# The mean square of y: two channel halves added on GpSimd ahead of the ones matmul

## The chip, the cores and the metric

The kernel runs on one core of a Trainium2 chip. The metric is the device time of one execution in microseconds (us); smaller is better. The core has five engines with queues of their own: TensorE (PE in the rows), VectorE (DVE), ScalarE (ACT), GpSimd (POOL) and SyncE (SP), which here issues transfers. Each works through its own list in order, and waits only where it meets a semaphore wait.

## The reference, cut to what matters

The input is 16 sequences of 512 tokens of 128 features. A layer with a state-space scan, a layernorm, a mixture of experts and a second layernorm follow one another. The change lies in the scan layer's own normalisation, the `rsqrt(mean(y * y))` below, a mean over 256 channels for each token:

```python
zxbcdt = x @ Win.T                         # z (256), xBC (512), dt (4)
xBC = silu(causal_conv4(xBC) + conv_b)     # x_ssm (256), B (128), C (128)
dtp = softplus(dt + dt_bias)
dA = exp(dtp * A)
# per token: h = dA * h + (dtp * x) outer B;  y = C . h + D * x
y = scan(...)                              # (b, 512, 256)
yn = y * rsqrt(mean(y * y, axis=-1, keepdims=True) + EPS) * norm_w
y = yn * silu(z)
x = layernorm(x + y @ Wout.T)
x = layernorm(x + moe(x))                  # 8 experts, top 2 of them per token
```

## The kernel before, in words

The program has a first part of about 510 us in which the sequences go through the scan layer and are sorted by expert, then the experts (`L575`, `L587` and others), then the last layernorm. Only the first part is touched.

It is a software pipeline over "slots", one per sequence `s`. A slot holds the scan of `s`, the projection and convolution of the next sequence `q`, the layernorm and routing of the one before, `r`, and the scatter of the rows of the one before that. Two slots at the start and four at the end are written out, and ten run in a hardware loop of two each. In a slot the work goes over `NC = 4` chunks `c` of 128 tokens. Every engine has its own function that writes its list for a slot: `slot_pe`, `slot_act`, `slot_dve`, `slot_pool`. The order on an engine is simply the order of that code.

Channels of y lie on the partitions, in `CC = 2` halves of 128, and tokens along the free axis: `yv` and `ysq` are [128, 2, tokens]. In chunk `c`:

- TensorE writes four heads' outputs to bank `p7` (L479, L485).
- VectorE adds the skip term and writes `yv` (L966). In the same row it does the conv taps (L794), the softplus steps on the small `sp` tiles (L812 to L832, spread over the chunks), the masked decay `M` (L856), `Xdt`, `carried` and `state`.
- ScalarE squares it to `ysq`: `square`, L638 to L642.
- GpSimd multiplies it by silu(z) to `gt`: `gate_y`, L1209 to L1215. It also makes `decayed` (L1238), `Xdd` (L1243) and `lhsA` (L1205, `expand`) for the scan, and issues one scatter of routed rows per chunk (L1221), whose descriptors it writes itself.

At the slot's end TensorE sums the squares over the channels: for each chunk, two matmuls of `ysq` halves with `ones`, accumulated in `p7` (L519 to L526). It then does the output projection from `gt` (L532) to `p5`, z (L408) and the projection of dt (L433). VectorE takes the mean of the squares to `ms` (L1010), after its gate steps `eg`, `gates`, top-8 and index. GpSimd raises `ms` to the power -1/2 (`rms`, L1262), issues four scatters more, and in the next slot does `lhsA` and then `rstd` (L1235), the layernorm's root. VectorE's `residual` (L878 to L900) waits for `rms` and the output projection.

Every float32 matmul shows in the trace as two passes, so that eight are x16.

Of the kernel before, what the change touches and what calls it, by code (L numbers as in the profile page):

```python
# [27 lines left out]
P = 128  # L28
SEQS, TOKS = 16, 512
NC = TOKS // P  # L30
H, HD = 4, 64
DI = H * HD
CC = DI // P
# [5 lines left out]
PADN = 96  # L39
# [28 lines left out]
def wait(eng, sem, value):  # L68

    if not isinstance(value, int) or value > 0:  # L70
        eng.wait_ge(sem, value)


def build(nc, t, out):
    ctx = ExitStack()
    with ctx:
        def sb(name, shape, dt=F32):
            return ctx.enter_context(nc.sbuf_tensor(name, shape, dt))
# [4 lines left out]
        def sem(name):  # L83
            return ctx.enter_context(nc.semaphore(name))
# [25 lines left out]
        ones = sb("ones", [P, P])  # L110
# [33 lines left out]
        carried = sb("carried", [P, DI])  # L144
        yv = [sb(f"yv{i}", [P, CC, P]) for i in range(2)]
        ysq = sb("ysq", [P, CC, TOKS])
        gt = sb("gt", [P, CC, TOKS])
        ms = sb("ms", [P, NC])
        rms = sb("rms", [P, NC])
# [82 lines left out]
        (x1_ready, Gm_ready, M_ready, Xdt_ready, v_ready, yv_ready, state_ready, sp_step, a_ready,  # L232
         tap_done, conv_done, carried_ready, ln_step, ve_ready, shift_ready, u_ready, gate_step, chosen_ready,
         ms_ready, pos_step, rank_read, slot_ready) = [sem(n) for n in names_dve]
        names_pool = ("lhsA_ready", "Xdd_ready", "decayed_ready", "g_ready", "rms_ready", "rstd_ready")
        (lhsA_ready, Xdd_ready, decayed_ready, g_ready, rms_ready, rstd_ready) = [sem(n) for n in names_pool]
        scattered = [[sem(f"scattered_{'AB'[k]}{i}") for k in range(2)] for i in range(2)]
        table_step = sem("table_step")
        table_ready = sem("table_ready")
# [146 lines left out]
        def _(pe):  # L386
# [50 lines left out]
            def slot_pe(s, scan, project, route):  # L437
# [79 lines left out]
                                       start=True, stop=True)  # L517
                    mm.then_inc(sums_psum, 1)
                if scan:  # L519
                    pe.wait_ge(sq_done, NC * (s.n + 1))  # L520
                    pe.wait_ge(yv_ready, NC * (s.n + 1))
                    for c in range(NC):
                        for k in range(CC):
                            mm = pe.matmul(p7[:, c * PADN:(c + 1) * PADN], ysq[:, k, c * P:(c + 1) * P],
                                           ones[:, 0:PADN], start=(k == 0), stop=(k == CC - 1))
                    mm.then_inc(ss_psum, 1)  # L526
                if scan:
                    pe.wait_ge(g_ready, NC * (s.n + 1))
# [89 lines left out]
        def _(act):  # L618
# [18 lines left out]

            def square(s, c):  # L638
                act.wait_ge(yv_ready, NC * s.n + c + 1)
                wait(act, ss_psum, s.n)  # L640
                act.activation(ysq[:, :, c * P:(c + 1) * P], yv[c % 2][:, :, :],
                               ACT.Square).then_inc(sq_done, 1)  # L642

# [523 lines left out]
        def _(pool):  # L1167
# [41 lines left out]
            def gate_y(s, c):  # L1209
# [4 lines left out]
                pool.tensor_tensor(gt[:, :, c * P:(c + 1) * P], yv[c % 2][:, :, :],  # L1214
                                   sz[s.par][:, :, c * P:(c + 1) * P], ALU.mult).then_inc(g_ready, 1)  # L1215

            def scatter(q, c, k):

                if (c, k) == (0, 0):
                    wait_apart(pool, slot_ready, q.n + 1)  # L1220
                pool.indirect_dma_start(  # L1221
                    out=sorted_rows[:, :],
                    out_offset=bass.IndirectOffsetOnAxis(slot[q.par][:, c, k:k + 1], 0),
                    in_=(rowA, rowB)[k][q.par][:, c, :], in_offset=None).then_inc(scattered[q.par][k], 16)

            def slot_pool(s, scan, project, route):
# [4 lines left out]
                for c in range(NC):  # L1231
                    n = NC * s.n + c
                    if route and c == 0:
                        pool.wait_ge(ve_ready, r.n + 1)
                        pool.tensor_tensor(rstd[:, :], ve[:, :], neg_half[:, :], ALU.pow).then_inc(rstd_ready, 1)  # L1235
                    if scan and 0 < c < NC - 1:
                        pool.wait_ge(state_ready, (NC - 1) * s.n + c)
                        pool.tensor_tensor(heads(decayed[:, :]), heads(state[(c - 1) % 2][:, :]),  # L1238
                                           per_head(decays[s.par][:, 2, :], c), ALU.mult).then_inc(decayed_ready, 1)
                    if scan and c + 1 < NC:  # L1240
                        pool.wait_ge(Xdt_ready, n + 1)
                        wait(pool, state_psum, (NC - 1) * s.n + c - 1)
                        pool.tensor_tensor(heads(Xdd[c % 2][:, :]), heads(Xdt[c % 2][:, :]),  # L1243
                                           per_head(decays[s.par][:, 1, :], c), ALU.mult).then_inc(Xdd_ready, 1)
                    if c > 0 and scan and (c + 2 < NC or project):
                        if c + 2 >= NC:
                            pool.wait_ge(a_ready, q.n + 1)
                        expand(n + 2, c + 2, s.par if c + 2 < NC else q.par)
                    if scan and c > 0:
                        gate_y(s, c - 1)  # L1250
                    if scatters:
                        scatter(s.plus(-2), c, 0)
                if project and not scan:
                    pool.wait_ge(a_ready, 1)
                    expand(0, 0, 0)
                    expand(1, 1, 0)
                if scan:
                    gate_y(s, NC - 1)
                    pool.wait_ge(ms_ready, s.n + 1)
                    if not (isinstance(s.n, int) and s.n < 1):  # L1260
                        pool.wait_ge(x1_ready, NC * s.n)
                    pool.tensor_tensor(rms[:, :], ms[:, :], neg_half[:, :], ALU.pow).then_inc(rms_ready, 1)  # L1262
# [83 lines left out]
```

## Time and profile before

| | us |
|---|---|
| median of three runs | 887.83 (886.22 to 889.96) |
| the profiled execution, whole | 882.78 |
| its span, first to last instruction | 880.9 |

| engine | busy us | share of the span |
|---|---|---|
| TensorE, matmuls | 708.9 | 80% |
| VectorE | 673.7 | 76% |
| GpSimd | 507.1 | 58% |
| ScalarE | 475.2 | 54% |

Busy time is an average over the whole program. The mean granted clock of TensorE was 0.932 of full speed. A row of the timeline gives an instruction's start, its duration, its engine and line, and what it writes from what it reads; in brackets stand the idle time of the engine before it and what ended it. The duration counts from when an instruction began to be executed, so that one held up within its execution shows as long and not as waiting.

### The profile page before, as it was taken

To read this page: it belongs to the slowest core of one execution; us is meant where nothing else is said; L and a number is where in the kernel's file an instruction comes from. 1 tells how busy PE (TensorE), PEld (TensorE's weight loads), DVE (VectorE), ACT (ScalarE), POOL (GpSimd) and SP (SyncE) were. 2 spreads that over 40 slices of the span, in tenths; PEclk is the share of its full clock that TensorE was granted. 3 is DMA by queue.
4 is the path that set the end of the run, shared out by engine and by line. 5 is a ranking of instruction groups with operands and counts; after the bars stand their busy time and mean duration, and the time that the engine had idled before them with its cause. 6 is when DMAs were issued, how large, how long until landed. Compare 5 with 4: busy or idle time off the path is not lost.

```text
span 880.9 us, 22802 instructions
## 1 busy us (share of the span) xinstructions
PE 708.9 (80%) x5288; PEld 601.1 (68%) x5289; DVE 673.7 (76%) x2331; ACT 475.2 (54%) x1188; POOL 507.1 (58%) x555
## 2 busy tenths in 40 slices
PE   5799878889988887897888731999999999999500
PEld 2577657667766665675666531999999999999500
DVE  5489988998998898898889645666666666667485
ACT  2566557546646655664665410655555555555355
POOL 2245666666665766676665755355555555555464
PEclk8899999999999999999999965999999999999855
DMA  3700011011101101101110002222222222222297
GB/s 85 251 26 23 16 43 44 14 42 45 42 14 43 42 12 42 42 21 36 31 35 14 19 30 73 59 64 61 66 65 64 68 61 63 65 57 77 72 301 218
DMA packets 74781, 53.84 MB, mean 61 GB/s; under 512 B 9435, under 2 KB 70110, under 8 KB 74480
## 3 DMA queue, kind: packets, MB, share of 16 engines
q1 hardware_dynamic: 56400, 31.90, 13.1%
q0 software_dynamic: 8448, 16.93, 5.9%
q10 hardware_dynamic: 9888, 4.49, 1.8%
q8 instruction: 19, 0.31, 0.1%
q14 instruction: 26, 0.21, 0.1%
HBM read 31.11 MB, written 22.69 MB: 61 GB/s over the span
## 4 chain that ended last, share of the span: by engine, by line
PE 36%; POOL 27%; issue 20%; DVE 9%; ACT 2%; DMA 2%; DVEq 1%; ACTq 1%; SPq 1%; POOLq 1%
PE pl L575 14%; POOL sorted_rows L1221 12%; PE p L587 12%; POOL lhsA L1205 5%; POOL gt L1214 4%; PE pj L569 2%; POOL rstd L1235 2%; ACT sz L745 2%; DVE acc L794 1%; DVE M L856 1%; PE pl L416 1%; POOL Xdd L1243 1%; POOL rms L1262 1%; DVE sp L822 1%; PE p L479 1%
## 5 line engine op out<-in xcount | busy, mean ns | idle before, releaser
L1275 POOL DMA_INDIRECT moe_rows<-yv,xs x136 | 146.0, 1074 | 141.0 <-DVE yv L1096 118.9
L724 ACT ACTIVATE L<-pl,b_sb 128x128 f32<-128x128 f32 x544 | 155.4, 369 | 118.9 <-PE pl L575 118.9
L575 PE MATMUL pl<-Btok,M 128*128 128x128 f32 x1088 | 151.2, 282 | 1.1 <-DVE M L1084 0.5
L587 PE MATMUL p<-w,L 128*128 x1088 | 143.9, 275 | 1.3 <-ACT L L724 1.3
L794 DVE SCALAR_TENSOR_TENSOR acc<-pj,conv_w_sb,acc 128x511 f32<-128x511 f32 (+2 forms) x192 | 142.2, 741 | 2.2 <-ACT acc L666 0.8
L575 PEld LDWEIGHTS pl<-Btok,M 128*128 128x128 f32 x1088 | 133.7, 193 | 4.4 <-DVE M L1084 3.2
L587 PEld LDWEIGHTS p<-w,L 128*128 128x128 f32 x1088 | 132.4, 192 | 1.8 <-issue 1.8
L1221 POOL DMA_INDIRECT sorted_rows<-rowA,slot x64 | 66.5, 1038 | 58.0 <-DVE token_id L875 47.5
L1080 DVE COPY Btok<-pj 128x128 f32<-128x128 f32 x136 | 39.7, 292 | 78.2 <-PE pl L575 61.2
L666 ACT ACTIVATE acc<-pj,conv_b_sb,conv_w_sb 128x512 f32<-128x512 f32 x64 | 49.8, 778 | 86.6 <-PE pj L397 85.8
L1205 POOL TENSOR_TENSOR lhsA<-after,a 128x512 f32<-128x512 f32 x64 | 67.9, 1062 | 32.0 <-DVE a L836 20.0
L416 PE MATMUL pl<-upto,lhsA 128*128 128x128 f32 x512 | 73.4, 290 | 0.8 <-POOL lhsA L1205 0.8
L1221 POOL DMA_INDIRECT sorted_rows<-rowB,slot x64 | 63.6, 994 | 18.0 <-issue 18.0
L397 PE MATMUL pj<-xT,w_xbc 128*128 128x512 f32 x128 | 69.1, 624 | 3.7 <-DVE acc L794 3.7
L416 PEld LDWEIGHTS pl<-upto,lhsA 128*128 128x128 f32 x512 | 67.9, 203 | 3.0 <-POOL lhsA L1205 1.6
L479 PEld LDWEIGHTS p<-M,Xdt 128*64 128x64 f32 x512 | 27.3, 136 | 60.4 <-issue 37.9
L631 ACT ACTIVATE L<-pl 128x512 f32<-128x512 f32 x64 | 38.2, 597 | 45.7 <-PE pl L416 44.5
L569 PE MATMUL pj<-ident,xs 128*128 128x128 f32 x136 | 40.1, 295 | 23.3 <-DMA xs<-sorted_rows 20.8
L1084 DVE COPY M<-w 128x512 f32 x136 | 57.2, 421 | 0.2 <-issue 0.2
L468 PE MATMUL p<-state,xc 128*128 128x256 f32 x96 | 33.5, 433 | 29.0 <-DVE state L976 23.3
L1214 POOL TENSOR_TENSOR gt<-yv,sz 128x256 f32<-128x256 f32 x64 | 53.3, 833 | 5.2 <-DVE yv L966 4.8
L856 DVE TENSOR_TENSOR M<-L,Gm 128x512 f32<-128x512 f32 x64 | 50.9, 795 | 2.0 <-ACT L L631 0.9
(170 smaller groups left out, 1477.3 us busy)
## 6 DMA issues: line engine op xcount, KB each, us to landing
xs<-sorted_rows SPq DMA_DIRECT2D x136, 65.0 KB, 1.8
xa<-in_x SPq DMA_DIRECT2D x16, 256.0 KB, 3.4
xres<-in_x SPq DMA_DIRECT2D x16, 256.0 KB, 3.0
w<-in_w SPq DMA_DIRECT2D x2, 2048.0 KB, 10.0
acc<-moe_rows SPq DMA_DIRECT2D x16, 256.0 KB, 3.9
xc<-moe_rows SPq DMA_DIRECT2D x16, 256.0 KB, 4.9
out<-sz ACTq DMA_DIRECT2D x16, 256.0 KB, 4.9
moe_rows<-yv,xs POOLq DMA_INDIRECT x136, 2.3
```

Of the source, the lines that this page charges most:

```text
L397: pe.matmul(pj[k % 2][:, :], w_xbc[:, k * P:(k + 1) * P], xT[q.par][:, :], start=True, stop=True).then_inc(proj_psum, 1)
L416: mm = pe.matmul(pl[c % 2][:, h * P:(h + 1) * P], lhsA[c % 2][:, h, :], upto[:, :], start=True, stop=True)
L569: pe.transpose(pj[k % 2][:, 0:P], xs[k][:, 0:P], ident[:, :]).then_inc(sT_psum, 1)
L575: mm = pe.matmul(pl[k % 2][:, f * P:(f + 1) * P], w1e[k % 2][:, f * P:(f + 1) * P], sT[k % 2][:, :], start=True, stop=True)
L587: mm = pe.matmul(o[:, 0:P], hT[k % 2][:, f, :], w2[:, bass.ds(e, 1), f, :].rearrange("p e d -> p (e d)"), start=(f == 0), stop=(f == FB - 1))
L724: act.activation(hT[k % 2][:, f, :], pl[k % 2][:, f * P:(f + 1) * P], ACT.Gelu, bias=b1[:, bass.ds(e * FB + f, 1)]).then_inc(hT_ready, 1)
L794: ins = dve.scalar_tensor_tensor(out=acc[:, k, j:TOKS], in0=pj[k % 2][:, 0:TOKS - j], scalar=conv_w[:, k, TAPS - 1 - j:TAPS - j], in1=acc[ ...
L856: dve.tensor_tensor(M[c % 2][:, :, :], L[c % 2][:, :, :], Gm[:, c, :].unsqueeze(1).broadcast_to([P, H, P]), ALU.mult).then_inc(M_ready, 1)
L1205: pool.tensor_tensor(lhsA[c % 2][:, :, :], after[:, :].unsqueeze(1).broadcast_to([P, H, P]), a[par][:, (c % NC) * H:(c % NC + 1) * H].unsq ...
L1214: pool.tensor_tensor(gt[:, :, c * P:(c + 1) * P], yv[c % 2][:, :, :], sz[s.par][:, :, c * P:(c + 1) * P], ALU.mult).then_inc(g_ready, 1)
L1221: pool.indirect_dma_start(out=sorted_rows[:, :], out_offset=bass.IndirectOffsetOnAxis(slot[q.par][:, c, k:k + 1], 0), in_=(rowA, rowB)[k][ ...
L1275: pool.indirect_dma_start(out=moe_rows[:, :], out_offset=bass.IndirectOffsetOnAxis(xs[k][:, P:P + 1].bitcast(I32), 0), in_=ye[k % 4], in_o ...
```

## The change

A new tile `ysum` holds the sum of the two halves of `ysq`. GpSimd makes it, one add of 128x128 per chunk (`add_halves`). It waits for the square of that chunk, and for TensorE to have read the `ysum` of the sequence before. In chunks 1 to 3 the add of the chunk before comes after `gate_y` and ahead of the scatter; for the last chunk it comes ahead of `gate_y`. TensorE has one matmul per chunk over `ysum` in place of two over `ysq`, and waits for GpSimd's semaphore instead of ScalarE's. `square` waits until GpSimd has read the `ysq` of the sequence before. Lines behind the new code have moved by 1 to 8.

```diff
@@ slot_pe
                 if scan:
-                    pe.wait_ge(sq_done, NC * (s.n + 1))
+                    pe.wait_ge(sq_sum, NC * (s.n + 1))
                     pe.wait_ge(yv_ready, NC * (s.n + 1))
                     for c in range(NC):
-                        for k in range(CC):
-                            mm = pe.matmul(p7[:, c * PADN:(c + 1) * PADN], ysq[:, k, c * P:(c + 1) * P],
-                                           ones[:, 0:PADN], start=(k == 0), stop=(k == CC - 1))
+                        mm = pe.matmul(p7[:, c * PADN:(c + 1) * PADN], ysum[:, c * P:(c + 1) * P],
+                                       ones[:, 0:PADN], start=True, stop=True)
                     mm.then_inc(ss_psum, 1)
@@ square
-                wait(act, ss_psum, s.n)
+                wait(act, sq_sum, NC * (s.n - 1) + c + 1)
@@ gpsimd
+            def add_halves(s, c):
+                tok = slice(c * P, (c + 1) * P)
+                pool.wait_ge(sq_done, NC * s.n + c + 1)
+                wait(pool, ss_psum, s.n)
+                pool.tensor_tensor(ysum[:, tok], ysq[:, 0, tok], ysq[:, 1, tok], ALU.add).then_inc(sq_sum, 1)
+
...
                     if scan and c > 0:
                         gate_y(s, c - 1)
+                        add_halves(s, c - 1)
                     if scatters:
                         scatter(s.plus(-2), c, 0)
...
                 if scan:
+                    add_halves(s, NC - 1)
                     gate_y(s, NC - 1)
```

GpSimd's list before, from chunk 1 of a slot in the loop to the end of that slot. `decayed`, `Xdd` and `lhsA` belong to the scan, `gt` is y gated, and the DMA is a scatter:

```order
L1238 TENSOR_TENSOR decayed<-state,decays 128x256
L1241 REGISTER_ALU
L1243 TENSOR_TENSOR Xdd<-Xdt,decays 128x256
L1205 TENSOR_TENSOR lhsA<-after,a 128x512
L1212 ISA
L1214 TENSOR_TENSOR gt<-yv,sz 128x2x128
L1221 DMA sorted_rows<-rowA,slot 67584x130
...
L1205 TENSOR_TENSOR lhsA<-after,a 128x512
L1214 TENSOR_TENSOR gt<-yv,sz 128x2x128
L1221 DMA sorted_rows<-rowA,slot 67584x130
L1214 TENSOR_TENSOR gt<-yv,sz 128x2x128
L1262 TENSOR_TENSOR rms<-ms,neg_half 128x4
```

The same part of GpSimd's list now:

```order
L1244 TENSOR_TENSOR decayed<-state,decays 128x256
L1247 REGISTER_ALU
L1249 TENSOR_TENSOR Xdd<-Xdt,decays 128x256
L1205 TENSOR_TENSOR lhsA<-after,a 128x512
L1212 ISA
L1214 TENSOR_TENSOR gt<-yv,sz 128x2x128
L1221 TENSOR_TENSOR ysum<-ysq 128x128
L1227 DMA sorted_rows<-rowA,slot 67584x130
...
L1227 DMA sorted_rows<-rowA,slot 67584x130
L1221 TENSOR_TENSOR ysum<-ysq 128x128
L1214 TENSOR_TENSOR gt<-yv,sz 128x2x128
L1270 TENSOR_TENSOR rms<-ms,neg_half 128x4
```

In each of chunks 1 to 3 `ysum` stands between `gt` and the scatter, and at the end it stands between the last scatter and the last `gt`. Nothing else changes place on GpSimd. TensorE's list at the end of a slot, before:

```order
L516 MATMUL p<-a,ones 128x96
L524 MATMUL p<-ones,ysq 128x96 x8
L532 MATMUL p<-w_out,gt 128x128 x8
L407 REGISTER_ALU
L408 MATMUL pj<-xT,w_z 128x512
```

and now:

```order
L517 MATMUL p<-a,ones 128x96
L524 MATMUL p<-ones,ysum 128x96 x4
L532 MATMUL p<-w_out,gt 128x128 x8
L408 REGISTER_ALU
L409 MATMUL pj<-xT,w_z 128x512
```

Eight matmuls have become four in the same place. VectorE's list is the same as before.

## Rows read from the trace of the kernel before

**Rows 1.** Busy us of each engine, 113 to 485 us: span, PE, PEld, DVE, ACT, POOL
```profile
113.00:485.00 372.00, 317.53 (x2227) 247.42 (x2226) 331.95 (x1079) 217.03 (x432) 247.31 (x277) 0.98 0.11 33
```

**Rows 2.** Timeline, end of one slot: start us, duration us, engine, line, out<-in [idle before]
```profile
230.34 0.73 POOL L1214 TENSOR_TENSOR gt<-yv,sz 128x256 f32<-128x256 f32 x1
...
231.24 1.01 POOL L1221 DMA_INDIRECT sorted_rows<-rowA,slot  x1 [0.17 <-issue]
...
232.07 0.42 ACT L641 ACTIVATE ysq<-yv 128x256 f32<-128x256 f32 x1 [0.61 <-DVE yv L966]
...
232.28 0.74 POOL L1214 TENSOR_TENSOR gt<-yv,sz 128x256 f32<-128x256 f32 x1
...
232.58 1.99 PE L524 MATMUL p<-ones,ysq 128*128 128x96 f32 x16
232.61 0.46 DVE L989 TENSOR_SCALAR eg<-eg 128x32 f32<-128x32 f32 x1
...
235.57 0.14 DVE L1010 TENSOR_SCALAR ms<-p 128x4 f32<-128x4 f32 x1
...
235.79 1.04 POOL L1262 TENSOR_TENSOR rms<-ms,neg_half 128x4 f32<-128x4 f32 x1 [2.77 <-DVE ms L1010]
...
236.21 1.02 PE L408 MATMUL pj<-xT,w_z 128*128 128x512 f32 x2
```

**Rows 3.** The chain of waits, one sequence later: start us, us, what
```profile
274.28 1.05 POOL rstd L1235
```

**Rows 4.** One line's instructions: duration in ns, min/median/max, first and last start
```profile
L1289 POOL TENSOR_TENSOR xc<-acc x8: 453/456/843, 835.2 to 865.8; 128x128 f32<-128x128 f32 x8
```

**Rows 5.** Timeline, chunk 1 and the start of chunk 2 of the slot of rows 2
```profile
217.05 1.06 POOL L1221 DMA_INDIRECT sorted_rows<-rowA,slot  x1 [3.31 <-DVE token_id L875]
...
217.66 0.42 DVE L820 TENSOR_SCALAR sp<-sp 128x16 f32<-128x16 f32 x1
...
218.29 2.07 DVE L822 SCALAR_TENSOR_TENSOR sp<-sp 128x16 f32<-128x16 f32 x1
...
219.28 1.04 POOL L1205 TENSOR_TENSOR lhsA<-after,a 128x512 f32<-128x512 f32 x1
...
220.28 1.27 POOL L1214 TENSOR_TENSOR gt<-yv,sz 128x256 f32<-128x256 f32 x1
...
220.89 0.69 DVE L822 SCALAR_TENSOR_TENSOR sp<-sp 128x16 f32<-128x16 f32 x1
...
222.16 0.16 DVE L822 SCALAR_TENSOR_TENSOR sp<-sp 128x16 f32<-128x16 f32 x1
...
223.86 0.60 POOL L1238 TENSOR_TENSOR decayed<-state,decays 128x256 f32<-128x256 f32 x1 [1.14 <-DVE state L976]
```

**Rows 6.** Timeline, chunk 1 of another slot, VectorE
```profile
280.39 2.83 DVE L820 TENSOR_SCALAR sp<-sp 128x16 f32<-128x16 f32 x1
```

**Rows 7.** Timeline, chunk 0 of two slots
```profile
210.34 0.69 DVE L856 TENSOR_TENSOR M<-L,Gm 128x512 f32<-128x512 f32 x1
...
211.11 1.05 POOL L1205 TENSOR_TENSOR lhsA<-after,a 128x512 f32<-128x512 f32 x1
...
213.98 0.69 PE L493 MATMUL p<-Xdd,Btok 128*128 128x256 f32 x2 [1.78 <-POOL Xdd L1243]
...
241.69 1.83 DVE L856 TENSOR_TENSOR M<-L,Gm 128x512 f32<-128x512 f32 x1 [0.24 <-ACT L L631]
```

**Rows 8.** Timeline, end of the last sequence
```profile
508.17 0.17 DVE L989 TENSOR_SCALAR eg<-eg 128x32 f32<-128x32 f32 x1
...
508.34 0.71 POOL L1214 TENSOR_TENSOR gt<-yv,sz 128x256 f32<-128x256 f32 x1 [0.40 <-DVE yv L966]
508.37 0.35 DVE L994 RECIPROCAL gates<-eg 128x32 f32<-128x32 f32 x1
...
510.82 0.16 DVE L1010 TENSOR_SCALAR ms<-p 128x4 f32<-128x4 f32 x1 [0.86 <-PE p L524]
```

**Rows 9.** Busy us as in rows 1 in one microsecond; the last but two is the granted clock
```profile
215.00:216.00 1.00, 1.00 (x6) 1.00 (x6) 0.93 (x9) 0.45 (x2) 0.00 (x0) 0.50 0.00 0
```

More of the change, by code:

```diff
@@ L146, in build @@
         ysq = sb("ysq", [P, CC, TOKS])
+        ysum = sb("ysum", [P, TOKS])
         gt = sb("gt", [P, CC, TOKS])
@@ L234, in build @@
          ms_ready, pos_step, rank_read, slot_ready) = [sem(n) for n in names_dve]
-        names_pool = ("lhsA_ready", "Xdd_ready", "decayed_ready", "g_ready", "rms_ready", "rstd_ready")
-        (lhsA_ready, Xdd_ready, decayed_ready, g_ready, rms_ready, rstd_ready) = [sem(n) for n in names_pool]
+        names_pool = ("sq_sum", "lhsA_ready", "Xdd_ready", "decayed_ready", "g_ready", "rms_ready", "rstd_ready")
+        (sq_sum, lhsA_ready, Xdd_ready, decayed_ready, g_ready, rms_ready, rstd_ready) = [sem(n) for n in names_pool]
         scattered = [[sem(f"scattered_{'AB'[k]}{i}") for k in range(2)] for i in range(2)]
```

## The prediction

> **What bounds the kernel now.** I first read the busy time by stretch. In the scan, over the twelve sequences from 113 to 485 us, VectorE is busy 331.95 of 372 us, TensorE 317.53 and GpSimd 247.31 [rows 1]. So a removed matmul need not pay, and added GpSimd work looks cheap; only the order in time can tell. I therefore read the end of a sequence, then its chunk 1.
>
> The last ones matmuls of a sequence (L524) start at 232.58 and take 1.99 us, until 234.57. VectorE, which consumes their sum in `ms` (L1010), starts that at 235.57, a full microsecond later: it is in an unbroken row of conv taps and gate steps, of which `eg` at 232.61 is one. GpSimd then starts `rms` at 235.79, having been idle 2.77 us [rows 2]. So TensorE's sum is not what is late; VectorE's own row is. Behind `rms` the chain of waits runs on GpSimd without a hole: after `rms` come four scatters and `lhsA`, and then `rstd`, in the next sequence at 274.28 [rows 3]. When `ms` comes sets when all of this comes. The next two outputs, z and the projection of dt, hang on TensorE, but in the next chunk 0 it waits 1.78 us for GpSimd's `Xdd` anyway [rows 7].
>
> **The change part by part.** I follow the sequence whose `rms` starts at 235.79.
>
> *Removed from TensorE.* Half of 16 passes in 1.99 us: 0.124 us each, so 1.0 us per sequence, 16 us in all, where VectorE was 1.0 us behind [rows 2]. Price: nothing, except in the first and last sequence. In the last, `ms` did wait 0.86 us for L524 [rows 8]. There the sum now starts later by one add (about 0.5 us) and lasts 1.0 us less: 0.4 us to the good. In the first I take the same, an estimate from this row. Together -0.8 us.
>
> *Added to GpSimd.* 64 adds of 128x128. The nearest row is the add of two 128x128 tiles later in the program, 0.456 us [rows 4]; GpSimd's records overlap by some 0.04 us (`lhsA` ends at 220.32, `gt` starts at 220.28, rows 5), so each takes 0.41 us of its queue. From above, `gt` with twice the elements takes 0.73 us [rows 2]; I take the first, whose shape is the same. Behind each of the first three adds stands the scatter of that chunk, then the next chunk's `decayed`, `Xdd` and `lhsA`.
>
> *What the adds push on GpSimd.* After the add of chunk 0 `decayed` has 1.14 us of idle before it [rows 5], so nothing comes late there. In chunk 3 nothing is idle: `gt` at 230.34 becomes 230.72, as the add of chunk 1 precedes it. It ends at 231.45. The square of chunk 2 ends 0.61 us ahead of that of chunk 3, so at 231.46 [rows 2], and the add runs to 231.95. The scatter, which needs 0.17 us of issue and 1.01 us, runs from 232.09 to 233.10, the last add to 233.57 and the last `gt` to 234.27. The square that the last add needs ended at 232.49, so it is GpSimd's backlog that counts and not ScalarE.
>
> *What that does to the end.* The ones matmuls start at 233.65 in place of 232.58 and end at 234.64, as now. The out matmuls follow at 234.56, behind a `gt` that is done; z follows at 236.37 in place of 236.21. Residual needs both out (236.54) and `rms` (235.79 + 1.04 = 236.83), so `rms` still decides. GpSimd is free at 234.27 with `ms` due at 235.57: 1.3 of the 2.77 us of idle are left. TensorE gets a new hole of about 0.9 us ahead of the sum, which nobody waits for. The new waits are thus covered. If that cover were gone (an add of 0.73 us, so GpSimd later by 4 x 0.3 us), the sum would end at 235.8 and cost 0.3 us per sequence.
>
> *What the adds do to VectorE without any wait.* This is the part that the list of waits does not show. In chunk 1 a tiny `sp` step on 128x16 takes 2.07 us, where its kind takes 0.16. It starts at 218.29, beside GpSimd's `decayed`, and ends at 220.36, after `Xdd` and with the end of `lhsA` at 220.32. The next one, at 220.89, takes 0.69 us and ends at 221.58, with `gt` (221.55); and `gt` itself takes 1.27 instead of the 0.73 of rows 2, held by a VectorE operation in its turn [rows 5]. Ten of the sixteen sequences show the 2.07. In another, `sp` at 280.39 takes 2.83 us, until 283.22, through all four GpSimd operations from `decayed` to `gt` [rows 6]. So VectorE operations that read two SBUF tiles, or are of the copy and scalar kind, and GpSimd's tensor operations keep each other out. Taps and `yv`, which read PSUM, run at their usual 0.74 and 0.42 us beside GpSimd.
>
> The new add stands directly behind this `gt`, with `sp` waiting. At the border between two back-to-back GpSimd operations VectorE was passed over at `decayed`/`Xdd` and `Xdd`/`lhsA`, and let in at `lhsA`/`gt` [rows 5]; in the slot at 280 it was passed over at all three [rows 6]. If it is passed over here, `sp` ends 0.41 us later and with it the taps, `yv`, and VectorE's whole row down to `ms`; the little idle time that it has [rows 1] lies mostly ahead of chunk 1's `sp`, in chunk 0. If it is let in, the add lies beside the tap that follows `sp` and costs nothing. Bounds: 0 to 0.7 us. I take 0.41, since the short operations' borders were the ones that stayed shut. It applies in the fifteen sequences that have such `sp` steps: 15 x 0.41 = 6.2 us.
>
> The Trainium skill ("SBUF — State Buffer", section "Who interferes with whom") says that of the two engines "Whoever issues first gets the shared pair for the whole instruction", and that a VectorE operation with two SBUF inputs competes with a GpSimd operation that reads SBUF. The trace agrees on the kinds and the full blocking (2.07 us of rows 5). Taken as first come first served, it would give the add no right over an `sp` that has waited since 220.89, and the price would be zero; rows 6 speak against reading it so.
>
> At the end of the sequence the same lock is met by `eg` (L989): 0.46 us now, held until `gt` ends at 233.02 [rows 2], where 0.17 us is its bare time [rows 8]. In the changed kernel a scatter stands at 232.09 to 233.10 instead. A scalar-kind step that started 0.61 us into a scatter (217.66 against 217.05) was held to its end too, 0.42 us [rows 5], so I expect `eg` to end at 233.08, as now. The reciprocal behind it ran its 0.35 us inside a `gt` [rows 8] and is not held. Price 0, bounds -0.29 (`eg` gets through) to +1.2 (passed over until 234.27).
>
> **The sum.** +6.2 - 0.8 = +5.4 us. The profiled execution took 882.78 us (span 880.9), so 888.2; the median of the runs shown, 887.83, is 5.05 above it, and I forecast 893.2 on that scale. Everything behind 513 us is untouched.
>
> **Rivals.**
> *The add is hidden.* `sp` is let in ahead of it. Only -0.8 remains: 887.0. For it: the border `lhsA`/`gt`. Against: rows 6. The skill's rule above gives this time.
>
> *Faster.* `eg` gets through beside the scatter, VectorE's row shortens by 0.29 us in 14 sequences, and the add is hidden too: -4.1 - 0.8 = -4.9, 882.9. For it: the scatter starts only about 0.5 us before `eg`, earlier than in the held case. Against: it needs both, and TensorE, 0.16 us later than now, then presses on residual's other inputs.
>
> *A lost race in chunk 0.* `M` at 210.34 ends at 211.03, 0.08 us before `lhsA` at 211.11. Where `M` started at 241.69, only 0.22 us before `lhsA`, it took 1.83 us instead of 0.69, until 0.56 us behind `lhsA`'s 1.05, and GpSimd's `rstd` had to wait for it [rows 7]; four sequences have this. TensorE is 0.16 us later at z, and if G thereby comes late enough against GpSimd, most sequences pay about 0.5 us (those 0.56 less the usual overlap): some 10 more x 0.5 = 5 on top of the 5.4, or `eg` passed over to `gt`'s start (0.5 x 14 = 7): 898 to 901. Against: VectorE's row, later by 0.41, moves `rms` too, so TensorE is rather early by comparison.
>
> *TensorE's clock.* After the wait of 1.78 us for `Xdd` at 213.98 the granted clock read 0.50 at 215 to 216, the 1.2 GHz level [rows 7, 9]. Were the new 0.9 us hole to bring a fall, sum and out would take 3.0 us more per sequence, 2 of it past `rms`: +30 us on the forecast, 923. Against: the hole is half as long as that one, and TensorE has work on either side.
>
> **Chances.** Forecast 0.42, hidden 0.26, faster 0.12, lost race or `eg` 0.17, clock 0.03. The likeliest has its own range of 890 to 896. For all: 883 to 902. A difference of 0.5% (4.4 us) is about what a measurement of this kernel can tell from none: faster than 883.4 takes half of "faster" and a little of "hidden", 0.08; slower than 892.3 takes two thirds of the forecast, the race and the clock, 0.48; the rest is 0.44.
>
> **What would show it.** The `sp` after `M` in chunk 1 at 1.1 us instead of 0.69 (step right) or still 0.69 (hidden rival); the add at about 0.45 us; the last ones matmuls starting 1.1 us later against `yv`, still ahead of `ms`; GpSimd's idle before `rms` at 1.3 to 1.7 us instead of 2.77; `eg` at 0.4 to 0.5. From one `rms` to the next now 30.8 us, or 31.3; in the forecast 31.2 and 31.7. I am wrong if `ms` waits for TensorE in the middle sequences, if the period is unchanged, or if the granted clock of the scan falls.

## The result, and the profile after

| | before | changed |
|---|---|---|
| median | 887.36 us (886.22 to 889.96) | 898.97 us (898.64 to 899.57) |
| profiled execution, its span | 882.78, 880.9 us | 898.64, 896.7 us |
| mean granted clock | 0.932 | 0.929 |

The changed kernel is slower: ratio 1.0126, 95% interval 1.0106 to 1.0146, which is 11.6 us by the medians. The two profiled spans differ by 15.8 us, as that of before was at the low end of its runs. The forecast was +5.4 us, 893.2, with a whole range of 883 to 902 and a likeliest one of 890 to 896.

I cut each sequence (from the `rms` of the one before to its own) at two marks that every trace has: the starts of `decayed` in chunk 1 and in chunk 2. Summed over the twelve sequences from 3 to 14, counting the first as 0:

| stretch | before | changed | difference |
|---|---|---|---|
| `rms` to `decayed` of chunk 1 | 160.1 us | 162.5 | +2.35 |
| to `decayed` of chunk 2 | 69.4 | 73.6 | +4.22 |
| to the next `rms` | 143.2 | 149.7 | +6.51 |

These +13.1 us, 1.5 us in the other sequences and 1.3 us behind the scan make the 15.8. Each stretch has a cause of its own.

**The middle stretch** is the step that was forecast. Timeline of the changed kernel, chunk 1 and the start of chunk 2 of the slot whose `rms` comes at 242.16; the columns are as in rows 2:

```profile
224.11 0.63 POOL L1244 TENSOR_TENSOR decayed<-state,decays 128x256 f32<-128x256 f32 x1
...
224.26 2.75 DVE L822 SCALAR_TENSOR_TENSOR sp<-sp 128x16 f32<-128x16 f32 x1
...
226.25 0.72 POOL L1214 TENSOR_TENSOR gt<-yv,sz 128x256 f32<-128x256 f32 x1
...
226.93 0.68 DVE L856 TENSOR_TENSOR M<-L,Gm 128x512 f32<-128x512 f32 x1
226.94 0.98 POOL L1221 TENSOR_TENSOR ysum<-ysq 128x128 f32<-128x128 f32 x1
...
227.54 0.42 DVE L822 SCALAR_TENSOR_TENSOR sp<-sp 128x16 f32<-128x16 f32 x1
...
230.20 0.70 PE L469 MATMUL p<-state,xc 128*128 128x256 f32 x2 [2.37 <-DVE state L976]
230.24 0.60 POOL L1244 TENSOR_TENSOR decayed<-state,decays 128x256 f32<-128x256 f32 x1 [1.15 <-DVE state L976]
```

`sp` now takes 2.75 us, until 227.01, with the end of `gt` at 226.97. In rows 5 it took 2.07 and ended with `lhsA`. `M` then gets in ahead of the add, and it is the add that is held (0.98 us), as `gt` was before (1.27). In both kernels the second `sp` ends with the last operation of GpSimd's run, at 221.58 with `gt` before [rows 5] and now at 227.96 with the add (227.92), so VectorE's row is later by about the add's length. From `decayed` to `decayed` it is 6.13 us in all twelve sequences, where it was 5.73 in ten and longer already in two (5.81, and 6.28 with the `sp` of rows 6).

The row of TensorE is the one that I had not asked for. Its wait for `state` is 2.36 or 2.37 us in eleven of the twelve. In before it was at most 1.97, as in this row of that trace:

```profile
410.76 0.70 PE L468 MATMUL p<-state,xc 128*128 128x256 f32 x2 [1.97 <-DVE state L976]
```

**The last stretch** holds the largest sum. TensorE's rows from that wait on, first one slot earlier, then (behind the dots) in the slot shown above; after that the busy time of both by the microsecond, with the columns of rows 9, whose last but two is the granted clock:

```profile
197.21 0.70 PE L469 MATMUL p<-state,xc 128*128 128x256 f32 x2 [2.37 <-DVE state L976]
197.74 1.06 PE L398 MATMUL pj<-xT,w_xbc 128*128 128x512 f32 x2
198.73 1.12 PE L480 MATMUL p<-M,Xdt 128*64 128x128 f32 x8
199.78 1.23 PE L486 MATMUL p<-ident,carried 128*128 128x128 f32 x4
...
231.69 0.66 PE L480 MATMUL p<-M,Xdt 128*64 128x128 f32 x8
232.28 0.71 PE L486 MATMUL p<-ident,carried 128*128 128x128 f32 x4
```

```profile
198.00:199.00 1.00, 1.00 (x4) 0.27 (x4) 1.00 (x5) 0.16 (x1) 0.61 (x1) 0.80 0.00 0
199.00:200.00 1.00, 1.00 (x9) 0.67 (x8) 1.00 (x4) 1.00 (x3) 0.21 (x1) 0.50 0.00 0
...
232.00:233.00 1.00, 1.00 (x13) 0.83 (x8) 1.00 (x4) 1.00 (x3) 0.20 (x1) 1.00 0.00 0
```

The same hole of 2.37 us stands ahead of both. In one the clock then reads 0.50, the 1.2 GHz level, for some 3.4 us, and eight matmuls take 1.12 us instead of 0.66; in the other it stays at 1.00. The fall came in five of the twelve sequences. The last stretch of those is 13.25 to 13.50 us instead of 11.68 to 11.92: 1.57 each, 7.8 in all. In the profile of before no sequence has a fall in chunk 2.

Yet the clock fell there too, in five of the twelve sequences, each time between chunks 0 and 1, behind TensorE's waits for `M` or `Xdd`, as in rows 7 and 9. In three of the five it cost nothing (the sequence of rows 9 took 30.81 us, one without a fall 30.80); the other two are those whose middle stretch was longer already. The changed kernel has one fall in that place. It has six falls in all against five, and its mean clock is almost the same: the falls moved to where they cost time.

**The first stretch.** Timeline of a later slot, whose `rms` came at 273.62:

```profile
274.56 0.59 PE L409 MATMUL pj<-xT,w_z 128*128 128x512 f32 x1
...
278.44 0.69 DVE L908 TENSOR_TENSOR Gm<-p,upto 128x512 f32<-128x512 f32 x1 [0.20 <-PE p L449]
...
279.26 2.08 DVE L856 TENSOR_TENSOR M<-L,Gm 128x512 f32<-128x512 f32 x1
...
279.73 1.05 POOL L1205 TENSOR_TENSOR lhsA<-after,a 128x512 f32<-128x512 f32 x1
...
280.73 1.52 POOL L1241 TENSOR_TENSOR rstd<-ve,neg_half 128x4 f32<-128x4 f32 x1
```

z starts 0.94 us behind `rms`, where it was 0.42 [rows 2]. `Gm` waits for TensorE, and `M` starts 0.47 us ahead of `lhsA`, where it had 0.77 [rows 7]. It loses the contest with it: 2.08 us instead of 0.69, until 0.56 us behind `lhsA`'s end, and the stretch is 13.62 us instead of 13.15. Four sequences of before paid that, ten of the changed kernel do.

The end of the sequence in the first slot, and the end of the last sequence:

```profile
237.91 0.46 POOL L1221 TENSOR_TENSOR ysum<-ysq 128x128 f32<-128x128 f32 x1
...
238.53 1.01 POOL L1227 DMA_INDIRECT sorted_rows<-rowA,slot  x1 [0.15 <-issue]
...
238.98 0.53 DVE L989 TENSOR_SCALAR eg<-eg 128x32 f32<-128x32 f32 x1
...
239.56 0.47 POOL L1221 TENSOR_TENSOR ysum<-ysq 128x128 f32<-128x128 f32 x1
239.97 0.73 POOL L1214 TENSOR_TENSOR gt<-yv,sz 128x256 f32<-128x256 f32 x1
...
240.08 1.13 PE L524 MATMUL p<-ones,ysum 128*128 128x96 f32 x8 [0.97 <-POOL ysum L1221]
...
241.94 0.14 DVE L1010 TENSOR_SCALAR ms<-p 128x4 f32<-128x4 f32 x1
...
242.16 1.04 POOL L1270 TENSOR_TENSOR rms<-ms,neg_half 128x4 f32<-128x4 f32 x1 [1.46 <-DVE ms L1010]
...
525.36 0.16 DVE L1010 TENSOR_SCALAR ms<-p 128x4 f32<-128x4 f32 x1 [0.52 <-PE p L524]
```

Here the changed kernel is as forecast: the sum is ready at 241.21, `ms` does not wait for it, and GpSimd still has 1.46 us to spare. In the last sequence `ms` waits 0.52 us for TensorE instead of 0.86 [rows 8], but in a second execution of the changed kernel, below, it waits 0.86 again.

### The profile page after: what moved, and what is told of

The parts are those of the page before. It is cut to its first block, busy times and chain, and to the rows that moved or that the text cites. A ratio compares the mean times of both kernels' runs of the same rounds, so it can differ in the third digit from the quotient of the medians.

```text
span 896.7 us, 22670 instructions
## 1 busy us (share of the span) xinstructions
PE 702.8 (78%) x5160; PEld 588.9 (66%) x5161; DVE 689.6 (77%) x2331; ACT 476.2 (53%) x1188; POOL 537.9 (60%) x619
## 4 chain that ended last, share of the span: by engine, by line
PE 34%; POOL 28%; issue 21%; DVE 10%; ACT 3%; DMA 2%; DVEq 1%; ACTq 1%; SPq 1%; POOLq 1%
PE pl L575 14%; PE p L587 12%; POOL sorted_rows L1227 12%; POOL gt L1214 4%; POOL lhsA L1205 4%; POOL ysum L1221 3%; PE pj L569 2%; POOL rstd L1241 2%; ACT sz L745 2%; DVE M L856 1%; DVE acc L794 1%; POOL decayed L1244 1%; POOL rms L1270 1%; POOL Xdd L1249 1%; DVE sp L822 1%
## 5 line engine op out<-in xcount | busy, mean ns | idle before, releaser
L417 PE MATMUL pl<-upto,lhsA 128*128 128x128 f32 x512 | 70.6, 282 | 0.8 <-POOL lhsA L1205 0.8
L417 PEld LDWEIGHTS pl<-upto,lhsA 128*128 128x128 f32 x512 | 65.2, 196 | 2.9 <-POOL lhsA L1205 1.6
L856 DVE TENSOR_TENSOR M<-L,Gm 128x512 f32<-128x512 f32 x64 | 59.6, 931 | 2.0 <-DVE Gm L908 1.0
L480 PE MATMUL p<-M,Xdt 128*64 128x128 f32 x512 | 44.9, 298 | 18.0 <-DVE Xdt L933 17.2
```

What stands on the lines that cost most here:

```text
L417: mm = pe.matmul(pl[c % 2][:, h * P:(h + 1) * P], lhsA[c % 2][:, h, :], upto[:, :], start=True, stop=True)
L480: mm = pe.matmul(p7[half, (h // 2) * P:(h // 2 + 1) * P], Xdt[c % 2][:, h * HD:(h + 1) * HD], M[c % 2][:, h, :], start=(h < 2), stop=(c == ...
L856: dve.tensor_tensor(M[c % 2][:, :, :], L[c % 2][:, :, :], Gm[:, c, :].unsqueeze(1).broadcast_to([P, H, P]), ALU.mult).then_inc(M_ready, 1)
```

## The experiments

Each was timed beside the kernel before on the same chip. The first four shared a chip, on which before took 884.7 us.

**The adds without TensorE's part.** Against the changed kernel:

```diff
-                    pe.wait_ge(sq_sum, NC * (s.n + 1))
+                    pe.wait_ge(sq_done, NC * (s.n + 1))
-                        mm = pe.matmul(p7[:, c * PADN:(c + 1) * PADN], ysum[:, c * P:(c + 1) * P],
-                                       ones[:, 0:PADN], start=True, stop=True)
+                        for k in range(CC):
+                            mm = pe.matmul(p7[:, c * PADN:(c + 1) * PADN], ysq[:, k, c * P:(c + 1) * P],
+                                           ones[:, 0:PADN], start=(k == 0), stop=(k == CC - 1))
@@ square
+                wait(act, ss_psum, s.n)
```

> GpSimd makes the four adds per sequence as in the changed kernel, but nobody waits for them at the end: TensorE runs both ones matmuls per chunk over ysq, as before. Theory (the add holds VectorE's sp step at the shared port by 0.4 us in chunk 1, and the later state lengthens TensorE's hole in chunk 2, where its clock then falls): the chunk 1 step of 0.4 us per sequence is there, 893 if the clock does not fall in chunk 2 and up to 900 if it does; TensorE is not later at z, so M of chunk 0 does not lose against lhsA more often than in the kernel before. Rival (the loss comes from TensorE waiting for GpSimd at the end of a sequence): 887 to 889.

Measured 899.01 us, ratio 1.0128 (1.0086 to 1.0169): the whole loss without anything of TensorE's. `sp` is at 2.75 and the clock falls in chunk 2 in six sequences, the second among them. The first stretch was lost here too, as `M` in this row shows, with `lhsA` at 215.91:

```profile
215.30 2.23 DVE L858 TENSOR_TENSOR M<-L,Gm 128x512 f32<-128x512 f32 x1
```

So neither the new hole ahead of the ones matmuls nor TensorE's wait for GpSimd is the main cost. z still comes 0.49 us (where `eg` was held at the end of the sequence before) or 0.80 us (where it gets through) behind `rms`, as the output projection waits for the late last `gt`; TensorE's wait for the last add makes these 0.70 and 0.94 in the changed kernel.

**TensorE's part without the adds**, the sum over one half of `ysq`. Against the kernel before:

```diff
-                        for k in range(CC):
-                            mm = pe.matmul(p7[:, c * PADN:(c + 1) * PADN], ysq[:, k, c * P:(c + 1) * P],
-                                           ones[:, 0:PADN], start=(k == 0), stop=(k == CC - 1))
+                        mm = pe.matmul(p7[:, c * PADN:(c + 1) * PADN], ysq[:, 0, c * P:(c + 1) * P],
+                                       ones[:, 0:PADN], start=True, stop=True)
```

> No adds; TensorE runs the ones matmul over the first channel half alone, so the second half is left out of the mean square. Theory (TensorE's sum was 1 us ahead of VectorE): within 1 us of the kernel before, 886.5 to 888. Rival (less TensorE work lowers its clock or moves the race in chunk 0): 892 or more. Second rival (the matmuls did cost time): 880 or less, some 0.5 us per sequence.

Measured 884.94 us, ratio 0.9993 (0.9974 to 1.0013). Half of the ones matmuls gone is worth nothing, even with no add in the way.

**The add of chunk 0 moved behind the scatter of chunk 1**, in the changed kernel:

```diff
-                        add_halves(s, c - 1)
+                        if c != 1:
+                            add_halves(s, c - 1)
                     if scatters:
                         scatter(s.plus(-2), c, 0)
+                    if scan and c == 1:
+                        add_halves(s, 0)
```

> The changed kernel, with only the add of chunk 0 moved from ahead of chunk 1's scatter to behind it, so it is no longer in one run of tensor operations with decayed, Xdd, lhsA and gt. Theory: the sp step of chunk 1 falls from 2.75 to 2.07 us, decayed to decayed from 6.13 to 5.73 us, 6 us of the time are back (893), and if the longer hole is what brings the clock down in chunk 2, 7 more (886). Rival (the adds cost their time in GpSimd's queue, wherever they stand): 899 as the changed kernel.

Measured 890.8 us, ratio 1.0061 (1.0037 to 1.0084): about half of the loss is gone.

```profile
218.18 2.07 DVE L822 SCALAR_TENSOR_TENSOR sp<-sp 128x16 f32<-128x16 f32 x1
...
222.05 0.38 DVE L822 SCALAR_TENSOR_TENSOR sp<-sp 128x16 f32<-128x16 f32 x1
...
222.63 0.47 POOL L1221 TENSOR_TENSOR ysum<-ysq 128x128 f32<-128x128 f32 x1
...
223.89 1.22 PE L469 MATMUL p<-state,xc 128*128 128x256 f32 x2 [2.14 <-DVE state L976]
```

The long `sp` is back at 2.07. The middle stretch is 5.89 us, 0.16 above before, since a later `sp` takes 0.38 instead of 0.16; why, I did not find. The clock still fell in chunk 2 in three sequences, this one among them, behind holes of 2.14 and 2.15 us.

**TensorE kept busy in its chunk 2 hole**, in the changed kernel, and nothing else different:

```diff
@@ slot_pe, ahead of the wait for state
+                        if c == 2:
+                            pe.wait_ge(L_ready, n + 1)
+                            for _ in range(5):
+                                pe.matmul(pl[0][:, 0:P], ident[:, :], ident[:, :], start=True, stop=True)
```

> The changed kernel, with five float32 matmuls of 128 columns into an idle bank in TensorE's hole of chunk 2, ahead of its wait for the state. Their results are not used. Theory (in five of the sequences TensorE's clock falls to its lower level in chunk 2 for some 3.5 us, 1.3 to 1.6 us each): no fall there, the stretch from chunk 2's decayed to rms is 11.9 us in all sequences, 7 us less, 892. Rival (that stretch is longer because of GpSimd's backlog behind the adds): it stays at 13.3 to 13.5 in the same five, 899.

Measured 891.7 us, ratio 1.0065 (1.0042 to 1.0089). TensorE in the slot that answers to the first one, then the clock behind its hole:

```profile
224.07 1.28 PE L470 MATMUL pl<-ident 128*128 128x128 f32 x10
226.60 0.70 PE L474 MATMUL p<-state,xc 128*128 128x256 f32 x2 [1.25 <-DVE state L981]
```

```profile
228.00:229.00 1.00, 1.00 (x12) 0.75 (x12) 1.00 (x4) 0.81 (x2) 0.39 (x1) 1.00 0.00 0
229.00:230.00 1.00, 1.00 (x10) 0.95 (x9) 0.96 (x4) 0.78 (x2) 0.81 (x1) 1.00 0.00 0
```

The middle stretches sum to 73.3 us (73.6 in the changed kernel) and `M` is held as often, and yet half of the loss is gone. Only the last stretch is much shorter, at 11.68 to 11.92 us in all sequences but one (12.38). No fall came behind the filled hole; between chunks 0 and 1 there were six falls. This run tells the clock's share from the rest: idle work buys back 0.6%, some 5 us.

The next four ran on a second chip, where before took 888.49 us. In all four traces there VectorE and ScalarE stood still in chunk 0 of most sequences, as in these rows of the added-step kernel below:

```profile
184.56 0.69 DVE L909 TENSOR_TENSOR Gm<-p,upto 128x512 f32<-128x512 f32 x1 [1.80 <-remote]
...
184.66 0.60 ACT L632 ACTIVATE L<-pl 128x512 f32<-128x512 f32 x1 [2.84 <-remote]
```

With `M` behind `lhsA` from the start, the contest of the two did not take place. What released the engines isn't in the profile, and these runs say nothing on the first stretch.

**Chunk 3's scatter moved behind the last `gt`**, in the changed kernel, so that the last add and `gt` come earlier:

```diff
-                    if scatters:
+                    if scatters and (c + 1 < NC or not scan):
                         scatter(s.plus(-2), c, 0)
...
                     gate_y(s, NC - 1)
+                    if scatters:
+                        scatter(s.plus(-2), NC - 1, 0)
```

> The changed kernel, with chunk 3's scatter moved from ahead of the last add to behind the last gt, into GpSimd's idle time before rms. Theory (the last add and gt come late, so TensorE's z and G come up to 0.5 us later against rms, and M of chunk 0 loses the port to lhsA in every sequence): the last ones matmuls start 0.6 us earlier, M of chunk 0 starts at rms + 5.35 again and takes 0.69 us in the sequences outside the loop's end, rms to decayed 13.15 us there instead of 13.62: 3 us less, 896; but eg now meets the last add and gt instead of the scatter and may be held up to 0.7 us, which would take it back. Rival (M is late for another reason): rms to decayed stays 13.62, 899.

Measured 891.28 us, ratio 1.0033 (1.0012 to 1.0054) on that chip, with its question left open; it was run again on a third one, below.

**The moved add and the fill together.**

> The changed kernel with both: the add of chunk 0 behind chunk 1's scatter, and five idle float32 matmuls in TensorE's hole of chunk 2. Theory: the two losses are separate in kind but both are healed: decayed to decayed 5.9 us, then 11.7 to 11.9 to rms in all sequences, with only the lost race (6 x 0.5) and 0.15 us per sequence left over the kernel before: 3 us above it, 888 to 889. Rival (moving the add had its gain only through the clock): the same as with the filler alone, 892.

Measured 891.72 us, ratio 1.0031 (1.0004 to 1.0059). That is a smaller loss than either has alone, but this chip's traces lack the contest in chunk 0 and hold the pauses; whether the two cures add up this run doesn't tell.

**A step added on VectorE, in the kernel before**, with no GpSimd work added, ahead of the second tap of chunk 1:

```diff
+                    if scan and project and c == 1:
+                        dve.reciprocal(idle_out[:, :], ones[:, 0:48])
```

> The kernel before, without any add, with one idle reciprocal of 128x48 (about 0.4 us, reading one SBUF tile, so not held by GpSimd) on VectorE in chunk 1 ahead of the second tap. Theory (any delay of VectorE's row in chunk 1 makes the state later, lengthens TensorE's hole in chunk 2 and brings the clock down): 0.4 us per sequence, 6 us, and in addition granted clock 0.50 in chunk 2 in some sequences, 3 to 7 us more: 894 to 898. Rival (the fall needs GpSimd's work or TensorE's lesser work): 891, clock at 1.00 in chunk 2.

Measured 897.49 us, ratio 1.0096 (1.0066 to 1.0125). In seven sequences the middle stretch was 6.55 us, with `sp` held 2.6 to 2.7 us, in four only 5.3 to 5.4. The hole in chunk 2, which the step was to lengthen, was 0.4 to 1.0 us in all but one of the twelve; in that one it was 2.23 us, and the clock fell behind it. With the pauses above I can't tell what a late `state` alone does, and count this as inconclusive.

**Fills in two holes of the kernel before**, in chunks 0 and 2, five idle matmuls each:

```diff
+                        if c == 2:
+                            pe.wait_ge(L_ready, n + 1)
+                            for _ in range(5):
+                                pe.matmul(pl[0][:, 0:P], ident[:, :], ident[:, :], start=True, stop=True)
...
+                            if c == 0:
+                                for _ in range(5):
+                                    pe.matmul(pl[0][:, 0:P], ident[:, :], ident[:, :], start=True, stop=True)
```

> The kernel before, with five idle float32 matmuls in TensorE's hole of chunk 0 (ahead of its wait for Xdd) and five in that of chunk 2. Theory (the clock falls in chunk 1 in most sequences because of the hole in chunk 0, but there GpSimd and VectorE set the time): the granted clock stays at 1.00 in the scan, and the time hardly moves, 885 to 888 (0 to 3 us less). Rival: TensorE at half clock in chunk 1 does cost, 0.5 us or more per sequence, 880 or less.

Measured 894.99 us, ratio 1.0063 (1.0041 to 1.0086), slower. There was no costly fall to heal, and the clock still fell between chunks 0 and 1 in seven of the twelve sequences. In those TensorE had no idle time left ahead of its work on `state`, so I take it that the fill itself stood in the way; no run separates this from the pauses.

The last four shared a third chip, without such pauses, on which before took 886.19 us.

**Only the add of chunk 0**, put into the kernel before, its result unused:

```diff
+                        if c == 1:
+                            add_halves(s, c - 1)
@@ square
+                wait(act, sq_sum, s.n)
```

> The kernel before, with one add per sequence on GpSimd, that of chunk 0 in chunk 1 behind gt, its result unused; TensorE runs both ones matmuls as before. Theory: this add alone does the two things of chunk 1 and 2: sp 2.75 us, decayed to decayed 6.13 us (+0.4 per sequence, 6 us), TensorE's hole in chunk 2 at 2.37 us and its clock falling there in some sequences (+5 to 8 us); the last gt comes on time, so M of chunk 0 wins against lhsA as before. Together 11 to 13 us over the kernel before. Rival (each add costs about a quarter of the whole): 3 us.

Measured 895.84 us, ratio 1.0105 (1.0048 to 1.0162): sixteen adds, each of them 0.46 us long where nothing holds it, cost 9 us. Timeline, then the clock behind it:

```profile
220.18 2.75 DVE L824 SCALAR_TENSOR_TENSOR sp<-sp 128x16 f32<-128x16 f32 x1
...
226.12 0.70 PE L469 MATMUL p<-state,xc 128*128 128x256 f32 x2 [2.37 <-DVE state L978]
```

```profile
228.00:229.00 1.00, 1.00 (x9) 0.67 (x9) 1.00 (x3) 1.00 (x3) 0.29 (x1) 0.50 0.00 0
```

The middle stretch is 6.12 to 6.13 us in every sequence, and the clock fell in chunk 2 in four, at 1.4 us each. `M` in chunk 0 was held in the same four sequences as in before.

**Only the adds of chunks 1 to 3**, likewise unused:

```diff
+                        if c != 1:
+                            add_halves(s, c - 1)
...
+                    add_halves(s, NC - 1)
                     gate_y(s, NC - 1)
@@ square
+                wait(act, sq_sum, (NC - 1) * s.n)
```

> The kernel before, with the other three adds per sequence, those of chunks 1 to 3, results unused, and no add of chunk 0. Theory: decayed to decayed stays 5.73 us, TensorE's hole in chunk 2 at most 1.97 and no fall of its clock there; the last gt is late, so M of chunk 0 loses against lhsA in every second sequence (+0.48 in some 6), against which eg gets through in the same (-0.24): +1 to +3 us. Rival (each add costs a quarter): +9 us.

Measured 886.49 us, ratio 0.9987 (0.9953 to 1.0021): forty-eight adds at no cost that can be told from the spread.

```profile
219.38 2.07 DVE L824 SCALAR_TENSOR_TENSOR sp<-sp 128x16 f32<-128x16 f32 x1
...
224.91 0.70 PE L469 MATMUL p<-state,xc 128*128 128x256 f32 x2 [1.97 <-DVE state L978]
```

The middle stretch stays at 5.73 us but for one sequence, the hole is at most 1.97, and no clock fell in chunk 2. Two of these three adds stand directly behind `gt` too; what they lack is a waiting VectorE step. I had expected them to lose `M` in chunk 0; they did not. The last `gt` is as late as in the run with all the adds (GpSimd idle 1.45 us ahead of `rms`), but here `eg` was held at the end of every sequence, z is at 0.49 us behind `rms`, and `M` starts 5.35 behind it, as before. So a late `gt` alone does not lose the contest.

**The changed kernel once more**, beside these two:

> The changed kernel as it is, on the same chip as the two beside it: 11 to 14 us over the kernel before, with the clock falling in chunk 2 in about five sequences by every theory.

Measured 897.6 us, ratio 1.0124 (1.0065 to 1.0183). The profiled execution had falls in chunk 2 in three sequences instead of five, so one program can have different numbers of them.

**The moved scatter again.**

> The same as the run with chunk 3's scatter moved behind the last gt, since there VectorE and ScalarE stopped for 1.8 us and more in chunk 0 of each sequence, ahead of M, so that the race of M and lhsA did not take place. Where they do not stop: theory, M starts at rms + 5.35 outside the loop's end and takes 0.69 us, rms to decayed 13.15 us there; rival, 13.62 as in the changed kernel.

Measured 892.23 us, ratio 1.0057 (1.0035 to 1.0080).

```profile
277.39 0.69 DVE L856 TENSOR_TENSOR M<-L,Gm 128x512 f32<-128x512 f32 x1
...
278.13 1.05 POOL L1205 TENSOR_TENSOR lhsA<-after,a 128x512 f32<-128x512 f32 x1
```

With z at 0.06 to 0.37 us behind `rms`, `M` in chunk 0 is again at 0.69 us, and the first stretch is 13.1 us wherever that of before is. `sp` stays at 2.75 but for one sequence, and the clock fell in chunk 2 in three. That ties the first stretch to the late last add and `gt`: `eg` got through in five sequences here too, and `M` won all the same.

No version was faster than the kernel before. Of those with all four adds and the halved sum the nearest had a moved add, a moved scatter or a fill, 0.3 to 0.65% above it.

## Why the prediction was right and wrong

The time of 898.97 lies in the whole range, on the side forecast as likelier, but above the likeliest range, and the loss is 11.6 us where the sum gave 5.4. It is also where the rival "a lost race in chunk 0" put it (898 to 901), and this is luck: the race made less than a third of the loss, and most of what the sum lacked came from TensorE's clock, at a hole that no rival had looked at. Part by part:

- **TensorE's removal, worth nothing: right.** Half of the matmuls alone gave a ratio of 0.9993. The gain of 0.8 us at the two ends is not shown: `ms` in the last sequence waits 0.52 us in one execution of the changed kernel and 0.86 in the other, against 0.86 before, and the last stretch there differs by nearly a microsecond between the two (9.02 and 8.21 us).
- **The add and GpSimd's queue: right.** The add takes 0.46 to 0.47 us where nothing holds it. The ones matmuls start 2.10 us behind the start of the last `yv` (L966), where it was 0.97, against 1.1 forecast as the difference. GpSimd has 1.22 to 1.46 us left ahead of `rms` (1.3 forecast), and only the last `ms` waits for TensorE.
- **Chunk 1's `sp`, +0.41 us a sequence: right in size and mechanism, wrong in place.** I expected VectorE to be let in at the border `lhsA`/`gt` as in rows 5, and then passed over at `gt`/add, so that the second `sp` would take 1.1 us. The first `sp` was held over `gt` as well, 2.75 us, and the second took 0.42. In most sequences VectorE was let in only ahead of the last tensor operation of GpSimd's run: of `gt` before, of the add now. In a few it was held to the run's end, as in rows 6. The sum over sequences 2 to 15 is +5.0 us against +6.2, as the slot of rows 6 had its long `sp` already. The kernel with the add of chunk 0 alone has this step whole; the one with the other three adds has nothing of it.
- **`eg` at 0.4 to 0.5 us, price 0: half right.** It takes 0.53 in seven of the twelve sequences and 0.17 in five, starting 0.45 to 0.46 us into the scatter in both cases. At the end of sequences 3, 5, 7, 9 and 11 it gave 0.24 us each, within the bound of 0.29. What lets it through I can't say.
- **The last `gt` and z: undersized.** I had z 0.16 us later against `rms`. Where `eg` was held it is 0.28 later, and where it got through, `rms` is earlier by 0.24 and z 0.52 later against it. In these traces `M` in chunk 0 loses against `lhsA` where it starts 5.50 us or more behind `rms`, and wins at 5.32 to 5.37; in sequence 3 it started at 5.55, in 4, 6, 8, 10 and 12 at 5.64. These six lost 0.48 us each, 2.9 in all; sequence 14, whose first stretch was long in before while `M` was not, got 0.48 back. The rival "lost race", at 0.17 in the chances, came true in six sequences instead of ten, and `eg` gave back 1.2 us of it.
- **The clock: the step that failed.** The prediction's last sign of being wrong was a fall of the granted clock in the scan, and in chunk 2 it came. The prediction put the rival at the new hole at the sequence's end, where nothing happened (0.97 us, clock unchanged), and gave it 0.03. It then let the 0.41 us of chunk 1 pass on to `yv` and `state` without asking what TensorE does in the meantime. It waits for that `state`. Rows 7 and 9 had shown that a hole in the scan can be followed by the 0.50 level, and I looked at the holes that the change adds, not at the one that it lengthens. With that hole at 2.37 us in place of 1.97 came falls of 1.57 us each, three to six in the traces of the changed kernel and of all adds alone: 4.7 to 9.4 us, which holds the missing 5.8. Filling it took 0.6% off and left the other causes nearly as they were.

By the ratios against their own runs of before: chunk 0's add with all that follows it 9.3 us, the other three adds none that shows, and the rest of the 11, some 2 us, is what the whole has and its halves lack, the lost `M` less `eg`'s gain. That last item is smaller than the intervals and rests on the traces alone.

**What stays open.** Identical holes of 2.37 us are followed by a fall in some sequences and not in others, in one and the same execution, and I found nothing in the rows ahead that tells them apart. In the traces of before and of the kernel with adds 1 to 3 no hole in chunk 2 was longer than 1.97 us and none brought a fall; over all traces, of 66 holes above 2.1 us in that place (sequences 2 to 14) 22 did. But the length is not all of it. A hole of 1.94 us brought a fall in a sequence of the changed kernel whose clock had fallen already between chunks 0 and 1, and in the second sequence of the kernel with the adds alone a hole of 1.88 us brought one with no fall before it. Why the falls between chunks 0 and 1 became rarer in the changed kernel is open as well. Whether a late `state` without any GpSimd work does the same was tried and came out inconclusive.

## What to carry to other kernels

When a step makes an engine late, look at every engine that waits for the result and not only at the end of the chain: a wait on TensorE that grows by 0.4 us can cost 1.6 us behind it through the clock. Before giving GpSimd a small operation, look at what stands directly ahead of it and who is waiting: at the end of a back-to-back run of tensor operations that holds up a VectorE step, it lengthens the hold and costs its whole time and more, while the same operation where no VectorE step waits cost nothing here. A fall of the clock can be free in one place and costly in another; count them by place, as the mean clock does not show it. And a matmul removed from an engine that is not late buys nothing, whatever its busy share.

## What the runs showed of the hardware

- The VectorE step `sp`, which reads and writes SBUF, was mostly passed over at each border between back-to-back GpSimd tensor operations but the last: 2.07 us with four in the run, 2.75 us with five, for a step whose bare time is 0.16. In single sequences it was held to the end of the run: 2.83 us with four [rows 6], 3.18 us with five in the second execution of the changed kernel. The Trainium skill ("SBUF — State Buffer", section "Who interferes with whom") gives the pair to whoever issues first; read as a queue, that does not fit these rows.
- Starting first did not protect `M`: 0.61 us ahead of `lhsA` it took 2.23 us, and 0.74 us ahead it took 0.69. Its bare 0.69 us would have ended behind `lhsA`'s start in the first case, and ended ahead of it in the second.
- The granted clock fell to the 1.2 GHz level behind some of the 2.37 us holes and cost 1.57 us each time in the changed kernel and 1.4 in the one with the add of chunk 0 alone; two executions of one program had five and three such falls. Falls of the same length between chunks 0 and 1 cost nothing in three sequences of five of the kernel before.
- Five idle matmuls, 1.28 us on TensorE, took 0.6% off the changed kernel. With one such fill in chunk 0 and one in chunk 2 the kernel before was 0.6% slower; it had no falls in chunk 2.
